# Reordered bias sums, turned bias rows and two groups of layer-norm factors in an attention and expert kernel

## The reference

```python
def _L0_gnn_ref(x, spatial_encoding, edge_encoding, Wq, bq, Wk, bk, Wv, bv):
    q = x @ Wq.T + bq
    k = x @ Wk.T + bk
    v = x @ Wv.T + bv
    a = q @ k.T * scale + spatial_encoding + edge_encoding
    return jax.nn.softmax(a, axis=-1) @ v
...
def _moe_forward(x, router_w, router_b, w1, b1, wg, bg, wv, bv, w2, b2):
    scores = xf @ router_w + router_b
    probs = jax.nn.softmax(scores, axis=-1)
    topk_p, topk_i = jax.lax.top_k(probs, K)
    gates = jnp.zeros((T, E), xf.dtype).at[jnp.arange(T)[:, None], topk_i].set(topk_p)
    h = jnp.einsum('td,edh->teh', xf, w1) + b1[None]
    gated = jax.nn.silu(jnp.einsum('teh,ehf->tef', h, wg) + bg[None]) * (jnp.einsum('teh,ehf->tef', h, wv) + bv[None])
    y = jnp.einsum('tef,efd->ted', gated, w2) + b2[None]
    return jnp.einsum('ted,te->td', y, gates)
...
x = x + _L0_gnn_ref(_layernorm(x, axis=-1), adj, adj, Wq, bq, Wk, bk, Wv, bv)
x = x + _L0_ffn_ref(_layernorm(x, axis=-1)[None], router_w, ..., b2)[0]
```

## Time and profile before

| | |
|---|---|
| time, median of 3 runs | 442.31 us (441.28 to 445.01) |
| the profiled execution: own time | 441.74 us |
| its span (first to last instruction) | 439.8 us |
| PE busy | 390.9 us, 89% |
| DVE busy | 303.0 us, 69% |
| POOL busy | 273.4 us, 62% |
| ACT busy | 179.1 us, 41% |
| moved by DMA | 89.43 MB, mean 203 GB/s |

### The profile page before, as it was taken

One profiled execution on the slowest core, in us unless ns is written; L12 is line 12 of the kernel. 1 busy time (PEld: TensorE's weight loads), 2 busy tenths in 40 slices (PEclk: granted clock), 3 DMA queues, 4 the chain that ended last, 5 costly groups with the idle time before them and its releaser, 6 DMA issues.

```text
span 439.8 us, 8120 instructions
## 1 busy us (share of the span) xinstructions
PE 390.9 (89%) x2272; PEld 337.8 (77%) x2272; DVE 303.0 (69%) x733; ACT 179.1 (41%) x312; POOL 273.4 (62%) x289
## 2 busy tenths in 40 slices
PE   0798996899999999999989596799998999999980
PEld 0687886798998998898878374588887878888870
DVE  3586866667696797787887585576766666767654
ACT  1274582354545535535625243353322323323310
POOL 3424676862855965965857653298798660377771
PEclk9998999599999999999999789799999999999995
DMA  6863449298698697698578938633884742232245
GB/s 198 246 225 134 141 123 338 73 304 248 197 310 259 208 329 254 204 335 266 143 270 268 362 139 261 204 145 97 292 278 170 250 161 62 84 98 85 71 129 171
DMA packets 55149, 89.43 MB, mean 203 GB/s; under 512 B 5326, under 2 KB 35474, under 8 KB 54084
## 3 DMA queue, kind: packets, MB, share of 16 engines
q1 hardware_dynamic: 43204, 75.36, 52.4%
q10 hardware_dynamic: 9280, 8.00, 5.7%
q0 software_dynamic: 2624, 5.56, 4.2%
HBM read 56.13 MB, written 32.77 MB: 202 GB/s over the span
## 4 chain that ended last, share of the span: by engine, by line
PE 46%; DMA 18%; DVE 12%; POOL 12%; issue 8%; ACT 1%; POOLq 1%; SPq 0%; ACTq 0%; DVEq 0%
PE ps L1266 21%; PE ps L960 16%; DVE acc L1395 7%; DMA first_row<-in_L_ffn_bv 5%; POOL lo L578 5%; DMA xblk<-expert_rows 3%; DMA expert_out<-ysum 3%; POOL expert_rows L603 3%; PE ps L1300 2%; DMA x<-in_x 2%; DMA expert_rows<-xn_all,posi_all 2%; PE ps L1161 2%; PE ps L1242 1%; DMA picked<-expert_out,ypos_i 1%; POOL ln L350 1%
## 5 line engine op out<-in xcount | busy, mean ns | idle before, releaser
L578 POOL TENSOR_TENSOR lo<-raw,hi 128x512 fp32r<-128x512 f32 x62 | 80.6, 1331 | 62.5 <-DVE acc L1395 54.2
L1266 PE MATMUL ps<-weights,bT_hi 128*128 x232 | 72.2, 392 | 0.0
L960 PE MATMUL ps<-hi,w1T_lo 128*128 128x512 f32 x128 | 55.4, 432 | 0.3 <-DVE w1T_lo L1319 0.3
L960 PE MATMUL ps<-lo,w1T_hi 128*128 128x512 f32 x128 | 52.6, 411 | 0.0
L960 PE MATMUL ps<-hi,w1T_hi 128*128 128x512 f32 x128 | 52.5, 410 | 0.0
L1161 PE MATMUL ps<-v,pT_hi 128*128 128x256 f32 (+3 forms) x242 | 45.7, 290 | 4.7 <-DVE pT_lo L1319 4.7
L1266 PEld LDWEIGHTS ps<-weights,bT_hi 128*128 128x128 f32 x232 | 43.8, 189 | 7.6
L1266 PE MATMUL ps<-weights,bT_lo 128*128 x116 | 48.6, 419 | 1.1 <-issue 1.1
L1395 DVE SCALAR_TENSOR_TENSOR acc<-raw,b1T,acc 128x512 f32<-128x512 f32 x48 | 42.4, 884 | 1.5
L1266 PE MATMUL ps<-weights,gT_hi 128*128 x232 | 42.7, 282 | 0.0
L1715 DVE TENSOR_TENSOR ps<-ps,bias 128x512 f32<-128x512 f32 x29 | 20.3, 699 | 31.4 <-PE ps L1266 24.8
(11 more groups left out here) (216 smaller groups left out, 968.0 us busy)
## 6 DMA issues: line engine op xcount, KB each, us to landing
expert_rows<-zeros SPq DMA_DIRECT2D x11, 1024.0 KB, 10.2
raw<-in_L_ffn_wg SPq DMA_DIRECT2D x8, 1024.0 KB, 6.5
raw<-in_L_ffn_wv SPq DMA_DIRECT2D x8, 1024.0 KB, 7.3
products<-ring SPq DMA_DIRECT2D x28, 256.0 KB, 4.7
landed<-products SPq DMA_DIRECT2D x7, 1024.0 KB, 7.7
adj_sb<-in_adj SPq DMA_DIRECT2D x10, 677.0 KB
bias<-biases SPq DMA_DIRECT2D x8, 640.0 KB, 5.5
w1raw<-in_L_ffn_w SPq DMA_DIRECT2D x8, 512.0 KB, 5.6
```

The lines of the kernel that those rows point to most:

```text
L578: G.tensor_tensor(lo[j % RAWS][:, k, :], raw[j % RAWS][:, k, :], r32(hi[j % HIS][:, k, :]), ALU.subtract).then_inc(m_lo, 1)
L960: last = nc.tensor.matmul(o, a, b, start=begins and n == 0, stop=ends and n == len(m) - 1)
L1266: last = nc.tensor.matmul(o, stationary[i][:, k, :], part(e, ats[j] + k * width, width), start=n == 0, stop=n == len(m) - 1)
```

## The change

Five things change.

1. bk and bq are loaded as two rows of 128 each into bias_rows, turned by one PE transposition and copied to their places by VectorE.
2. The layer-norm factors are made in two groups (FACTORS): tiles 0 to 7 on VectorE after the second group of statistics, tiles 8 to 10 on GpSimd (finish_factors) after a rough value by VectorE.
3. load_first_row moves from SP's list to ScalarE's. Sum 0 is spread over t = 3 to 5 (two chunks, then one each), sum 1 over t = 6 to 9; the products of matrix 0 move from t = 6 and 8 to t = 7 (behind queries(1)) and 9.
4. In step 1 VectorE takes sum 4 at the end, behind add_mix(0); sum_hi(4), matrix_lo(4) and sum_lo(4) move into step 2. At the end, add_mix(10), the second layer norm and place_rest(7) come ahead of the first half of sum 15; place_tile(7) is cut in two.
5. On GpSimd scatter(8) comes ahead of count_tile(9). On SP load_weights(2) and load_down(2) move behind the loads of the first three row blocks. ScalarE's waits for all scatters and clears move behind its last keep_product. The output goes out in three stores where there were eleven.

```diff
+    FACTORS = [(0, 2 * PER), (2 * PER, TILES - 2 * PER)]
...
+        def finish_factors(wait_ge, engine, g, queue):
+            mean, _, var, y, tmp, shift = factors_of(g)
+            count = 14 * g
...
+            wait_ge(rough1, 2 * g + 2)
+            for _ in range(3):
+                step(engine.tensor_tensor(tmp, y, y, ALU.mult))
+                step(engine.tensor_tensor(tmp, tmp, var, ALU.mult))
+                step(engine.tensor_scalar(tmp, tmp, -0.5, 1.5, ALU.mult, ALU.add))
+                step(engine.tensor_tensor(y, tmp, y, ALU.mult))
+            step(engine.tensor_tensor(tmp, mean, y, ALU.mult))
+            step(engine.tensor_scalar(shift, tmp, -1.0, None, ALU.mult))
+            queue.sem_inc(factors_done)
...
# SyncE
-            sp.wait_ge(wqk_in, 48)
+            sp.wait_ge(wqk_in, 32)
...
-            for t in range(TILES):
-                n = width(t)
-                sp.wait_ge(added, t + 1)
-                sp.dma_start(out[span(t, n), :], x1[:n, t, :]).then_inc(result_out, 16)
+            for t in (0, HALF):
+                sp.wait_ge(added, t + HALF)
+                sp.dma_start(out[t * P:(t + HALF) * P, :].rearrange("(t p) d -> p t d", p=P), x1[:, t:t + HALF, :]
...
# GpSimd
-            for t in range(FIRST, TILES):
+            for t in range(FIRST, 2 * PER):
+                x_rows(t)
+            finish_factors(pool.wait_ge, G, 1, pool)
+            pool.wait_ge(factors_done, 2)
+            for t in range(2 * PER, TILES):
                 x_rows(t)
...
-                matrix_lo(s + 3)
-                sum_lo(s + 3)
+                if s == 2:
+                    matrix_lo(4)
+                    sum_lo(4)
+                if s > 1:
+                    matrix_lo(s + 3)
+                    sum_lo(s + 3)
...
+            scatter(TILES - 3)
             count_tile(TILES - 2)
-            for t in range(TILES - 3, TILES):
-                scatter(t)
+            scatter(TILES - 2)
+            scatter(TILES - 1)
# ScalarE
-                act.dma_start(wk_raw[:, :, D], bk.rearrange("(k p) -> p k", p=P)).then_inc(wqk_in, 16)
-                act.dma_start(bqk[:, 0, :], bq.rearrange("(k p) -> p k", p=P)).then_inc(bq_in, 16)
+            act.dma_start(bias_rows[0:KD, :], bk.rearrange("(k p) -> k p", p=P)).then_inc(bq_in, 16)
+            act.dma_start(bias_rows[KD:2 * KD, :], bq.rearrange("(k p) -> k p", p=P)).then_inc(bq_in, 16)
...
+                if s == 2:
+                    sum_hi(4)
...
-                if s == 1:
-                    sum_hi(3)
-                sum_hi(s + 3)
+                sum_hi(3 if s == 1 else s + 3)
+                if s + 3 < MATS - 1:
+                    load_first_row(4 if s == 1 else s + 4)
                 w1_hi(j // 2 + 1, j % 2, COMB)
...
+                if s == 1:
+                    load_first_row(5)
# TensorE
-            pe.wait_ge(wqk_in, 48)
-            pe.wait_ge(cleared, 5)
+            pe.wait_ge(bq_in, 32)
+            nc.tensor.transpose(ps[:, 7, TURNED_ROWS:TURNED_ROWS + 2 * KD], bias_rows[:, :], ident[:2 * KD, :2 * KD]
+                                ).then_inc(small_mm, 1)
+            pe.wait_ge(wqk_in, 32)
+            pe.wait_ge(cleared, 7)
# VectorE
-            for g in range(len(GROUPS)):
-                statistics(g)
-            factors()
+            statistics(0)
+            dve.wait_ge(small_mm, 1)
+            V.tensor_copy(wk_raw[:, :, D], ps[:, 7, 128:128 + KD]).then_inc(cleared, 1)
+            V.tensor_copy(bqk[:, 0, :], ps[:, 7, 128 + KD:128 + 2 * KD]).then_inc(cleared, 1)
+            statistics(1)
+            rough_factors(0)
+            finish_factors(dve.wait_ge, V, 0, dve)
...
+            statistics(2)
+            rough_factors(1)
...
                 if t == 3:
-                    gather_bias(0)
+                    gather_bias(0, (0, 1))
+                if t in (4, 5):
+                    gather_bias(0, (t - 2,))
+                if t in (6, 7, 8, 9):
+                    gather_bias(1, (t - 6,))
```

More of the change, by code:

```diff
@@ L352, in newton, with factors_of, step @@
                 engine.tensor_scalar(y, tmp, 1.5, y, ALU.add, ALU.mult).then_inc(newton2, 1)
+        def factors_of(g):
+            t0, n = FACTORS[g]
+            return [mv[:, t0:t0 + n, 0], mv[:, t0:t0 + n, 1]] + [rs[:, i, t0:t0 + n] for i in range(4)]
+        def finish_factors(wait_ge, engine, g, queue):
+            mean, _, var, y, tmp, shift = factors_of(g)
+            count = 14 * g
+            def step(ins):
+                nonlocal count
+                count += 1
+                ins.then_inc(newton1, 1)
+                wait_ge(newton1, count)
+            wait_ge(rough1, 2 * g + 2)
[7 more added lines that the diff above has]
+            queue.sem_inc(factors_done)
         PASSES = ((1, 0), (0, 1), (0, 0))
@@ L476, in _ @@
                     load_w1(j // 2 + 2)
-                if 0 < s and s + 4 < MATS:
-                    load_first_row(s + 4)
                 store_product(2 * j + 1)
@@ L514, in _ @@
                 sp.dma_start(xblk[:, i, :], xs[bass.ds(row, P), :]).then_inc(rows_in[i], 16)
+            load_weights(2)
+            load_down(2)
             load_bias(1)
@@ L883, in _ @@
             sum_hi(2)
+            load_first_row(3)
             keep_product(3)
@@ L1517, in place_tile @@
                 V.tensor_copy(posi_all[:n, t, :], pos_all[:n, t, :]).then_inc(posi_done, 1)
+            def place_tile(t):
+                place_first(t)
+                place_rest(t)
             def add_mix(t):
@@ L1598, in _ @@
             normalise2(TILES - 1)
+            place_rest(TILES - 4)
+            gather_bias(MATS - 1, range(KH // 2))
             choose(TILES - 2)
```

115 lines of the change are left out of this document (48 added, 67 removed).

## The result

The changed kernel takes 422.47 us (421.65 to 424.83), against 442.74 for the kernel before over the runs so far: ratio 0.9545, with a 95% interval of 0.9511 to 0.9579. That is 20.3 us less; the forecast was 415.6, 26.7 less than the 442.31 known then, and the range 410 to 424 holds the time. The profiled execution took 422.16 with a span of 420.4. A few executions came out over 1.5% above the fastest of the same kernel; they are in the medians and ranges of the experiments and left out of the ratios.

The account below looks back on a forecast made before the run. PE, busy 390.9 of 439.8 us, was taken as the bound, leaving waits and low-clock stretches to win; 3.2 + 1.9 + 8.5 + 1.1 + 12 = 26.7 off 441.74, plus 0.57, gave 415.6 us, range 410 to 424.

Parts of the forecast that it names:

- Start: Before PE's first transpositions: earlier layer-norm factors and biases loaded as rows save 3.2 us (1.76 to 3.74).
- t = 4: PE's wait for xT_lo behind sum 0's chunks, and its slow clock: spreading them saves 1.9 us (0 to 3.7).
- Step 1: PE's wait for pT_lo behind sum 4, and the slow clock after it: moving the sum saves 8.5 us (4.7 to 8.7).
- POOL has 97.90 - 67.32 = 30.6 to spare: GpSimd's idle time in the long window: work added to step 2 is paid back in two or three steps.
- Step 10: PE's wait for place_in: a first row arriving in time on ScalarE's queue saves 1.1 us (0 to 1.1).
- End: Around the end of step 11: earlier residual sum, scatters and landing, and better clock save 12 us (5.4 to 14.6).
- 2.6 for the scatters: Part of the end term: scatter(8) ahead of the count lets the last scatter issue 2.6 us earlier.
- The landing: Part of the end term: with two weight loads moved away, the last scatter's 6.99 us transfer shortens by 3.5.
- Behind the first block: Part of the end term: PE's 5.00 us at clock 0.59 there recover 1.0 us, half of up to 2.0.
- the waits only move: Rival, chance 0.13: at the end only the residual sum's move counts, 5.4 us; sum 20.1, time 422.2.
- The queue doesn't matter: Rival, chance 0.15: a first row takes 10.65 us whichever engine starts it; sum 24.4, time 417.9.
- Slower: Rival, chance 0.03: first-row loads in ScalarE's list hold w1_hi and the probabilities, making PE wait each step; time 448.6.

Follow-up runs that it names:

- rows_on_sp: Changed kernel with all first-row loads put back on SP's list: 426.29 us, ratio 0.9618 to the kernel before.
- count_first: Changed kernel with scatter(8) put back behind count_tile(9) on GpSimd: 423.08 us, ratio 0.9515 to the kernel before.
- lo_on_dve: Changed kernel with GpSimd's two chunks of matrix 15 moved to VectorE, behind place_tile(10): 419.91 us, ratio 0.9486 to the kernel before.
- weights_early: Changed kernel with load_weights(2) and load_down(2) put back ahead of the first three row blocks: 421.60 us, ratio 0.9525 to the kernel before.
- best: lo_on_dve's move on the changed kernel, plus sum 15 behind choose(10) and place_tile(9), first block's bT_lo behind the routing tables: 418.33 us.

## Why the prediction was right, and where it was wrong

The range holds the time, but partly by luck. The forecast by itself was said to run from 410.5 to about 420, and 422.47 lies outside that; it is inside the range because this was stretched to 424 for a rival. In the trace 19.4 were gained of the 26.7: the end gave less than forecast, 5.0 us were lost at three places where the sum had no loss or 0.2, and the start and t = 4, which came out 2.1 above their terms, made up for a part.

*Start: 3.2 forecast, 4.1 measured.* The mechanism was right, and in the traces both edits are needed for it. It came out above the upper end of 3.74, which allowed for the factors alone: Wq's product began 1.85 earlier and the 1.76 behind it went too, so that the first transposition came 3.9 earlier (13.45 against 17.39). Between it and tile 2, line 1030 took 1.03, where the same product took 1.84 before, and the new wait of 1.2 for bqk_each took that back: its VectorE instruction now stands behind the third group of statistics and its rough factors, and the prediction had the small operations of the biases as hidden. The row that ends at 9.62 was read as the first group of statistics; it is the second (the view has the first at 6.74 + 0.36 = 7.10), so the allowance until 9.62 does hold the second group.

*t = 4: 1.9 forecast, 3.1 measured.* Right in kind; the half that I left for one contended chunk did not come. The 3.1 itself is one trace against one, in a piece that varies by 2.7 between traces of the same lists, so a part of it may be chance.

*Ahead of the first mix: nothing forecast, 1.3 lost.* PE waits 1.0 for acc_lo on GpSimd there in the changed kernel, and the 1.3 are lost in every run here, also with sum 0 in one go and with the first rows on SP's queue. I had followed the moved sums on VectorE and not on GpSimd. Which of the moves ahead of it is the cause was not tried.

*Step 1: 8.5 forecast, 8.9 measured, but 2.3 lost in step 2, where I had left 0.2.* The step that failed is "POOL has 97.90 - 67.32 = 30.6 to spare", by which the moved matrix_lo(4) cost nothing. GpSimd had the time, but VectorE beside it had not: sum 5 ran at less than half its speed. With it came one of the prediction's own signs of being wrong, a wait for pT_lo in step 2 (0.7). The row for it was among mine, three chunks in 4.12; I took it as a matter of t = 3 alone.

*Step 10: 1.1 forecast, 1.3 measured.* Right: from the tenth mix to the eleventh it takes 14.1 before, 12.8 now and 14.3 in rows_on_sp, which loses it again.

*End: 12 forecast, 1.0 of it behind the first block; 7.0 measured up to the first block.* This is the term that was mis-sized, and its parts fared differently. The residual sum moved by 7.8, as forecast, and the last issue by 5.4. But in my sum 5.4 belonged to the order alone, and 2.6 for the scatters came on top, 8.0 at the last issue: count_first shows that the 2.6 is nothing. That the last issue came out at the other number, 5.4, is chance: choose(9) began 6.3 earlier against the mix (5.8 behind it, 12.1 before), 2.2 of this were lost by the last place of tile 10, on the way to which hot_all stood behind GpSimd's chunks, and 1.3 came back among the last scatters, for which no run gives the reason. The chunks' price is 2.9 at the first block by lo_on_dve. The landing went from 7.0 to 5.3, not to 3.5; the moved loads gave 1.4 of that by weights_early.

*Behind the first block: 1.0 forecast, 1.4 lost.* The granted clock of the first 5 us rose a little (0.68, against 0.59 before), but the wait ahead of the second block's products went from 1.1 to 2.1, with 0.66 behind it (265.9 to 270.9). The first five blocks take 21.2 instead of 19.0; a part comes back later. best takes this wait away, and its trace meets another.

Of the rivals, "the waits only move" (422.2) met the time best, though only in part for its reasons: 5.4 at the last issue is its number, and the scatters' order gave nothing, as it says; but the last landing was 1.7 faster than it has it, and the losses of 1.3, 2.3 and 1.4 at other places are not in it. "The queue doesn't matter" is refuted by rows_on_sp (12.4 against 4.3 for a row, 2.7 at the first block; 3.8 in the medians). "Slower" has nothing for it: no sum waits for its first row in the changed kernel, and PE's list of waits has none for the probabilities. Two slips change nothing: the waits that are said to lie at four places are named at five, and the 0.51 for an issue is, in rows 10, GpSimd's idle time ahead of a scatter; an issue of a first row on ScalarE's queue takes 0.23.

## What to carry to other kernels

Work moved to an engine with idle time is not free if another engine shares a resource with it: before GpSimd takes an elementwise product of two buffers, look at what VectorE does in the same microseconds, and price that at the contended rate that the trace already holds. Where GpSimd's instructions stand back to back, look for one VectorE instruction, small or large, that is held through the whole run. And two edits that act on the same wait need not add up: undo them singly and together before either gets the credit.

## What the runs showed of the hardware

A VectorE instruction on 128x8 numbers took 3.18 instead of 0.22 us, one on 74x8 3.19 instead of 0.17 and a chunk of 128x512 3.44 instead of 0.75, through a whole run of GpSimd instructions behind a scatter; in step 2, with no scatter about, chunks of 128x512 against one another went by turns instead, some 1.7 for 0.75 on VectorE and 1.7 for 1.26 on GpSimd. What decides between the two stays open. A transfer of one row of 2 KB took 4.3 us from issue to use on ScalarE's queue and 12.0 to 12.4 on SP's at the same place. The last scatter of best was issued 2 us earlier than that of lo_on_dve and took 2 us longer to land (7.11 against 5.17), so that its end did not move.
